# Matmuls into an unread PSUM bank in the Chebyshev tiles that have no expert pass beside them

## The reference, cut to what matters

```python
xn = _layernorm(x)
s  = windowed softmax attention(xn)        # 16 heads of 8, 64 keys back
g  = silu(ternary linear(xn))
x  = x + s * g
xn = _layernorm(x)
s  = _L1_attn_ref(xn)                      # Chebyshev linear attention
g  = silu(_L1_ffn_ref(xn))                 # top 2 of 8 experts, 128 -> 512 -> 128, then a layer norm
x  = x + s * g
```

## Time and profile before

| | |
|---|---|
| median of three runs | 874.4 us |
| their range | 871.69 to 875.07 us |
| the profiled execution, its time | 876.45 us |
| its span | 874.6 us |
| PE busy | 596.5 us (68%) |
| DVE busy | 660.3 us (75%) |
| ACT busy | 441.9 us (51%) |
| POOL busy | 436.9 us (50%) |
| mean granted clock of TensorE | 0.847 of full speed |

### The profile page before, as it was taken

How to read it: one execution, slowest core, us unless ns; L and a number is a source line. 1 busy time by engine, 2 the same in 40 slices (tenths; PEclk the granted TensorE clock), 3 DMA queues, 4 the chain that set the end, 5 groups by cost and what they waited for, 6 DMA issues and landing times.

```text
span 874.6 us, 22303 instructions
## 1 busy us (share of the span) xinstructions
PE 596.5 (68%) x7049; PEld 402.2 (46%) x7049; DVE 660.3 (75%) x1711; ACT 441.9 (51%) x1075; POOL 436.9 (50%) x697
## 2 busy tenths in 40 slices
PE   1898899998988988842327777777777775324220
PEld 0566666665655655520214555555555553112110
DVE  4688888888787677743845898899898898617777
ACT  1456555554544454410417787888888774101111
POOL 3145555555457677657703344444444343764721
PEclk9999999998999799965658999999999997555555
DMA  9999999200000000001121232323232321111211
GB/s 228 345 283 287 286 288 287 75 0 0 0 8 18 15 18 18 16 13 45 48 76 38 85 99 93 102 81 104 85 100 85 96 69 41 52 45 36 66 31 36
DMA packets 127372, 80.93 MB, mean 93 GB/s; under 512 B 11832, under 2 KB 118208, under 8 KB 127296
## 3 DMA queue, kind: packets, MB, share of 16 engines
q1 hardware_dynamic: 122160, 70.97, 27.2%
q0 software_dynamic: 5136, 9.02, 3.8%
HBM read 18.85 MB, written 49.55 MB: 78 GB/s over the span
## 4 chain that ended last, share of the span: by engine, by line
PE 34%; DVE 33%; issue 17%; POOL 7%; ACT 4%; SPq 1%; DVEq 1%; DMA 1%; another core or an unknown queue 1%; POOLq 0%; ACTq 0%
PE m_ps L1047 5%; PE e_ps L1059 4%; DVE yts L1394 3%; POOL experts_sb L563 3%; DVE mneg L1142 3%; PE y_ps L1010 2%; PE q_ps L954 2%; PE m_ps L823 2%; PE p_ps L1003 2%; DVE pr L1391 2%; PE y_ps L887 2%; DVE pr L1393 2%; ACT pexp L610 2%; DVE rot L1184 2%; PE m_ps L837 2%
## 5 line engine op out<-in xcount | busy, mean ns | idle before, releaser
L610 ACT ACTIVATE pexp<-e_ps 128x512 f32<-128x512 f32 x128 | 76.5, 598 | 75.4 <-PE e_ps L870 66.7
L1142 DVE TENSOR_REDUCE mneg<-m_ps 128x4 bf16<-128x512 f32 x128 | 84.7, 683 | 22.5 <-PE m_ps L837 22.2
L1047 PE MATMUL m_ps<-xs,wb 128*128 128x512 f16 x276 | 80.4, 403 | 19.8 <-issue 18.6
L563 POOL DMA_INDIRECT experts_sb<-ybuf,slots x64 | 63.5, 993 | 32.3 <-issue 18.9
L492 POOL DMA_INDIRECT xbuf<-x,slots x64 | 65.2, 1019 | 16.6 <-issue 14.9
L1019 PE MATMUL p_ps<-eye_sb,yn 128*128 128x128 f32 x32 | 11.6, 363 | 80.4 <-DVE yn L1399 64.2
L887 PE MATMUL y_ps<-pexp,vd 128*32 128x128 f32 x512 | 57.6, 295 | 3.1 <-ACT pexp L610 1.0
L557 POOL TENSOR_TENSOR pexp<-rot,pexp 128x512 f16<-128x512 f32 x24 | 27.8, 1157 | 56.6 <-ACT pexp L731 56.6
L851 PE MATMUL e_ps<-early 128*128 128x256 bf16 x256 | 52.0, 284 | 0.1
L557 POOL TENSOR_TENSOR pexp<-qt,pexp 128x512 f16<-128x512 f32 x24 | 30.3, 1264 | 43.1 <-ACT pexp L731 43.1
L1101 PE MATMUL e_ps<-b_sb,cwt 8*128 8x128 f32 x64 | 16.6, 436 | 49.3 <-ACT cwt L780 49.3
(11 more groups left out here) (223 smaller groups left out, 2129.7 us busy)
## 6 DMA issues: line engine op xcount, KB each, us to landing
xbuf<-zero_sb SPq DMA_DIRECT2D x71, 256.0 KB, 4.0
ybuf<-zero_sb SPq DMA_DIRECT2D x71, 256.0 KB, 3.6
wb<-experts_sb SPq DMA_DIRECT2D x46, 256.0 KB, 2.3
xs<-xbuf SPq DMA_DIRECT2D x23, 256.0 KB, 2.7
ybuf<-vd SPq DMA_DIRECT2D x23, 256.0 KB, 2.2
experts_sb<-in_experts_w SPq DMA_DIRECT2D x8, 512.0 KB, 6.9
x_all<-in_x SPq DMA_DIRECT2D x8, 256.0 KB, 5.3
xbuf<-x,slots POOLq DMA_INDIRECT x64
```

The lines of the kernel that those rows point to most:

```text
L563: nc.gpsimd.indirect_dma_start(yg[:, 2 * (B * n + b) + k, :], None, ybuf, bass.IndirectOffsetOnAxis(ap=slots[:, k, B * n + b:B * n + b + 1 ...
L610: nc.scalar.activation(pexp[:, j, :, :], e_ps[j % 2][:, :, :], ACT.Exp, scale=float(D) ** -0.5).then_inc(exp_ready.sem, 1)
L1047: last = nc.tensor.matmul(u_ps[f % 2], wb1[:, i % 2, f, a, :], xg16[:, i % 2, b, :], start=k == 0, stop=k == len(PARTS) - 1)
L1142: nc.vector.tensor_reduce(mneg[:, n.batch, j // 2, (j % 2) * NG:(j % 2) * NG + NG], m_ps[j % 2][:, :, :], AX.X, ALU.max, negate=True).then ...
```

## The change

PE gets a new function, `fill(c)`. In the tiles c = 0 to 3 (i from -4 to -1) and c = 27 to 31 (i = 23 to 27), and once more behind the loop (c = NT), it multiplies twelve times a 128x128 matrix of ones by the 128x512 matrix winm_sb, both bfloat16, into u_ps[1]. Nothing reads these products. For i >= 0 it first waits for the last gelu of the last pass; for i < 0 it waits for nothing. It stands right before `transpose_out(c - 1)` in PE's order; in c = 3 that is behind `transpose_rows(0)`. No other engine's instructions change.

```diff
+            def fill(c):
+
+                i = c - LEAD
+                if i < 0 or i >= PASSES:
+                    after(pe, s_gelu, 2 * FB * PASSES if i >= 0 else 0)
+                    for k in range(12):
+                        nc.tensor.matmul(u_ps[1], onesb_sb[:, :], winm_sb[:, :, :], start=True, stop=True)
+
             def transpose_rows(i):
...
                 if i == -1:
                     transpose_rows(0)
+                fill(c)
                 if c:
                     transpose_out(c - 1)
                 up(i + 1, 0)
...
                 down(i, 3)
+            fill(NT)
             transpose_out(NT - 1)
             project_out(NT - 1)
```

## The result

The kernel after the change took 892.61 us, the median of four runs (887.93 to 893.18 us). The kernel before, run beside it, took 874.74 us (871.69 to 876.86 us, four runs). The ratio is 1.0195, with a 95% interval of 1.0149 to 1.0241: slower by 17.9 us. The prediction was 872.7 us with a range up to 878.5, so the result lies outside it, on the side that had a chance of 0.12, and beyond both prices of the rival on that side (880.5 and 887).

A forecast was written before the change was run, and what follows sets the result against it. DVE was taken as busy in the passes and, at the loop's ends, waiting for PE's low-clock matmuls. Terms -2.1 + 3.2 + 0 - 2.8 = -1.7 us, so 872.7 us against the median of 874.4; range 866.5 to 878.5.

The forecast's parts named there:

- the rival on that side: Rival 1, the slower side: priced at 880.5 us, or 887 if no fill were ever warm; chance together 0.12.
- rival 3: Tail, 757 to 781 us: DVE's unexplained late steps, some 15 us, go away; priced at 862 us, chance 0.12.
- DVE's end counts in the tail: From tile 27 on, POOL later waits 12.91 us for DVE, so up to 12.9 us gained by DVE shortens the kernel.
- The clock: Granted clock near 1.00 from 420 to 440 and 728 to 755 us; a warm fill takes 2.6 us.
- Tiles 0 to 2: Head: DVE's waits before `clip`, 0.83 and 1.25 us, both go; a gain of 2.1 us, bounds 0 and 2.1.
- Tile 3: Fill behind `transpose_rows(0)` delays the first pass by 4.2 us, 1.0 comes back; a loss of 3.2 us.
- Tiles 4 and on: No fill there; clock falls may vanish (-4.0 us) or one more come (+1.7); taken as 0.
- Rival 2: Tile 3's fill raises the clock before `up(0, 0)` and later falls vanish: -4.0 us more, 868.7 us, chance 0.17.
- Tiles 27 to 31: Tail: high clock holds, DVE's waits of 1.30 and 1.46 us go; a gain of 2.8 us, bounds 0 and 3.9.
- its chance of 0.59 for "the same": Forecast of 872.7 us together with rival 4, that the change does nothing, within about 0.5% of before: 0.59.
- Rival 1: Clock high for the fill, low again for the work: tiles 0 to 2 and 27 to 29 gain nothing; 880.5 us.

The follow-up runs named there:

- recorded comparison: The first comparison: changed kernel, four runs, against the kernel before, four runs beside it; 892.61 against 874.74 us, ratio 1.0195.
- undisturbed: Profiles of the later sets, without the waits laid to "remote"; the kernel before had medians of 856.6 to 858.1 us there.
- 17 later profiles: Profiles from the five later sets of runs, on four chips, of the kernel before, the changed kernel and edited versions; set medians of the kernel before 856.6 to 858.1 us.
- experiment with 4 groups ahead: Kernel before with 4 groups of gathers, not 5, ahead of `deviation(0)`: 854.12 us (0.9965); with fills of tiles 0 to 2 and the tail too: 847.20 us (0.9896).
- the three comparisons: Changed kernel, unedited, rerun against the kernel before in three later sets: 857.08, 856.21 and 856.10 us; ratios 1.0003, 0.9985 and 0.9986.
- the 56 matmuls ahead of the rows: Kernel before plus fills of tiles 0 to 2 and 56 matmuls ahead of `transpose_rows(0)`: 853.34 us (0.9947); without the 56, 853.83 us (0.9956).

## Why the prediction was wrong, and where it was right

Two steps failed. The first is the term that the sum did not have: the trace of before held starts of DVE that were late without a cause, some 15 us in all, and the sum took them over as they stood, while rival 3 let them only shrink. In the recorded comparison such late starts came more heavily instead: +5.0 us where tiles 0 to 2 were to give -2.1, and +10.4 us where tiles 27 to 31 were to give -2.8. The second is a premise that fails undisturbed too: that DVE's end counts in the tail. POOL's 40 gathers end last there.

**The clock.** Right where it was reckoned, and in part beyond. The forecast was 1.00 where the sums of tile 0 begin, and a warm fill at 2.6 us; measured 1.00 and 2.75 us for twelve. It was to be near 1.00 from 420 to 440 and from 728 to 755 us; measured 0.83 and 0.88 in the recorded profile, 0.82 and 0.94 in the undisturbed one (before 0.67 and 0.67). Rows and the rule of the Trainium skill ("TensorE: Matmul & The Clock Gate", Back-to-back issue gap) were to be told apart here: twelve at its 131 ns would be 1.6 us, an estimate. The trace does not agree with it; the row's 0.215 us stands.

**Tiles 0 to 2, forecast -2.1 us.** Right in size. In the undisturbed profiles the stretch from the second clip ahead of the loop to the rows' arrival is 40.73 us before (413.57 to 454.30) and 38.30 after (409.69 to 447.99): -2.4. Over all 17 later profiles it is 40.7 to 41.9 us in the six without the fills' work there and 38.3 to 39.9 in the eleven with it. The two runs with these fills alone gave -3.8 and -2.8 us by the medians (854.25 against 858.05, 853.83 against 856.61). But not both of DVE's waits always go: in five of the eleven, the clip of tile 2 still waits 1.0 to 1.7 us. In the recorded profile this same stretch is 5.0 us longer, with 12.7 us of ACT's idle time before the three copies, not all of it on the path.

**Tile 3, forecast +3.2 us.** Right. The fill was 4.68 and 4.92 us where 4.2 was reckoned. From the rows' arrival to the clip of tile 5 it is +2.7 us in the recorded profiles and +2.1 in the undisturbed ones, and the run with this fill alone gave +2.6 us (1.0031). In the six later profiles with this fill that stretch is 10.9 to 11.5 us, in the five without any fill of the head at work 9.1 to 9.3. As forecast, the delay is PE doing its work in program order, with part of it given back.

**Tiles 4 and on, forecast 0.** Right within what chance moves: from the clip of tile 5 to the first gather -0.6 us in the recorded pair, +1.0 in the undisturbed one (265.18 and 266.14). Rival 2, that the passes inherit the high clock, fell: the clip of tile 6 still waits 4.03 us in the undisturbed profile after, and 3.00 in the one before.

**Tiles 27 to 31, forecast -2.8 us.** Wrong in its premise, even where nothing disturbs. The failed words are "its end is what counts there", said of DVE, with "up to 12.9 us that DVE gains there are gained by the kernel". The tail did become faster at `combine(0)`, by 6.0 us, more than reckoned, although one of the two waits meant to go, that of tile 28's clip, only shrank to 0.87 us. But the wait of 12.91 us before `deviation(0)` belonged to the disturbance in the profiled execution of before (the late stretch that rival 3 named); without it POOL waits for nobody, and the 40 gathers hide the gain: 0.9998 for the tail's fills alone. The experiment with 4 groups ahead shows the same from the other side. There the fills of head and tail are worth 6.9 us, and from the first gather to `deviation(0)` they bring 45.4 down to 41.0.

**The sum.** Against an undisturbed kernel before, the steps as measured are -2.4 + 2.1 + 1.0 + 0 = +0.7 us; the three comparisons gave ratios of 0.9985 to 1.0003, none of which differs from 1 by 0.5%. The forecast's own ratio, 872.7 / 874.4 = 0.998, and its chance of 0.59 for "the same" fit these, in part by luck, as a gain of 2.8 us that did not exist stood in the sum; they did not fit the recorded comparison. Nor can a single pair of profiles check such a sum: the first layer, which is the same code in all kernels, brings the second clip anywhere from 407.7 to 413.6 us in the 17 later profiles.

**The recorded +17.9 us.** The profile's marks place it: +2.7 us in tile 3, which was foreseen, and the rest in the two stretches with the late starts of ACT, above all one of 27.5 us in the tail. None of the rivals had them. Rival 1 named the right sign with another mechanism, the clock falling between a fill and the work behind it. That fall does occur: from 742 to 746 us the recorded profile has 0.57, and the undisturbed one ran tile 28 at the low clock. But it cost 0.87 us at that tile's clip, no fill of the undisturbed tail overran its wait, and the undisturbed kernel is no slower, so it is not where the 17.9 us went. The nearest was rival 3: the trace of before held a late stretch without a cause (11.01 us and some 15 in all), and I priced that it might go, to 862, and not that it might come more heavily. A stall that nothing in the profile explains can move both ways, and belonged into both ends of the range. With it went the base: 874.4 us, too, was a time with the stall in it. Undisturbed, the same kernel takes 857.

**What stays open** is the cause of these waits, and whether the change had a part in their being longer. For an outer cause: they occur in both recorded kernels, in the first layer too, and in none of the 17 later profiles, which come from four chips. Which chip the recorded comparison ran on is not on record, so the chip itself is not excluded either. Against an outer cause alone: all four recorded runs of the changed kernel lay at 888 to 893 and all of the kernel before at 872 to 877, so under whatever held there, the changed kernel was the one that lost more. That the two only met the waits at different instants (ACT's one long wait ended when the gathers had drained) was argued, not shown. Against an instruction load that came late speaks the view of DMA queues: from 775 to 795 us, around the end of that wait, it shows packets of the gathers' queue alone. Whether that view holds ACT's loads is not shown.

```profile
q0 software_dynamic: 416, 0.85, 16.1%
```

## What to carry to other kernels

Here the added matmuls paid where a later engine waits for a matmul that they speed up through the clock, and only there: before adding such matmuls, find the join behind them and see which engine comes last to it, here 40 gathers that nobody had counted. Do not place them behind a wait for data on PE's own queue, for the data's first use then waits for them (2 to 3 us here). Ahead of it, 56 of them that ended 3.12 us before the data came brought nothing that could be measured; whether ones that last until it comes would help was not tried. And where a profile shows a wait of 10 us with no cause, take a second profile of the unchanged kernel before reasoning from it: the premise of this prediction's tail, and its base, were both of that wait.

## What the runs showed of the hardware that was not expected

- In one comparison ACT stood up to 29 us, 27.5 of them with its input complete and no releaser in the profile; in 17 other profiles of nearly the same code it never did. Each of the long waits fell where indirect transfers were running or had just ended; a stream of plain writes beside them, 320 GB/s, did not bring it on in a later set.
- The same kernel took 874.7 us in one comparison and 856.6 to 858.1 us in five others.
- After 3.12 us without work (the 56 matmuls ahead of the rows) PE's granted clock was still high for a row transpose (0.62 us) and low for the first product 2.0 us later (1.46 us for three matmuls), although 12.25 us of unbroken work lay before the gap.
